# Eight heads to a value product, a 96-column shift product, and a new order of the work, in a four-layer cross-attention kernel

## The reference, cut to what matters

```python
x = _L0_xattn_ref(ctx, x, ...)        # causal attention 0, cross 1, relu feed-forward
x = _L1_xattn_ref(x, ctx, ...)        # causal attention 2, cross 3, experts
x = _L2_xattn_ref(x, ctx, mask, ...)  # masked attention 4, cross 5, relu feed-forward
x = _L3_xattn_ref(x, ctx, ...)        # cross attention 6
# one attention:
scores = jnp.einsum('bhqd,bhkd->bhqk', q, k) / np.sqrt(HEAD_DIM).astype(np.float32)
if mask is not None:
    scores = jnp.where(mask == 0, NEG, scores)
attn = jax.nn.softmax(scores, axis=-1)
out = jnp.einsum('bhqk,bhkd->bhqd', attn, v)
```

## Time and profile before

| | us |
|---|---|
| median of 3 runs | 3417.2 (3404.26 to 3429.27) |
| profiled execution | 3387.68 |
| its span, first to last instruction | 3385.9 |
| PE busy in the span | 3120.8 |
| DVE busy | 1568.8 |
| ACT busy | 1541.6 |
| POOL busy | 872.8 |
| mean granted clock | 0.951 |

### The profile page before, as it was taken

One profiled execution on the slowest core, in us unless ns is written; L12 is line 12 of the kernel. 1 busy time (PEld: TensorE's weight loads), 2 busy tenths in 40 slices (PEclk: granted clock), 3 DMA queues, 4 the chain that ended last, 5 costly groups with the idle time before them and its releaser, 6 DMA issues. The chain is left out here.

```text
span 3385.9 us, 61962 instructions
## 1 busy us (share of the span) xinstructions
PE 3120.8 (92%) x24016; PEld 2469.1 (73%) x24016; DVE 1568.8 (46%) x4051; ACT 1541.6 (46%) x3403; POOL 872.8 (26%) x991
## 2 busy tenths in 40 slices
PE   6899998999999999975999999789999999999996
PEld 5777776777877777764888888657676776777774
DVE  4544556645566555443100010275555555655542
ACT  3555455555556554442222222245555554555542
POOL 2112214222224222322000000332243433343332
PEclk8999999999999999995999999899999999999996
DMA  9725436455454453742766655553354565453321
GB/s 159 104 40 66 56 49 105 67 71 67 64 74 80 70 67 59 168 77 105 231 220 211 204 198 195 103 82 48 54 76 59 64 77 69 63 80 59 52 54 28
DMA packets 394608, 319.35 MB, mean 94 GB/s; under 512 B 151711, under 2 KB 378271, under 8 KB 394303
## 3 DMA queue, kind: packets, MB, share of 16 engines
q1 hardware_dynamic: 371062, 276.77, 46.7%
q0 software_dynamic: 8272, 23.73, 2.6%
q10 hardware_dynamic: 14981, 14.89, 1.4%
HBM read 134.33 MB, written 37.22 MB: 51 GB/s over the span
## 5 line engine op out<-in xcount | busy, mean ns | idle before, releaser
L1067 DVE TENSOR_REDUCE a_maxima<-a_bank 128x2 f32<-128x512 f32 (+3 forms) x576 | 342.4, 646 | 159.6 <-PE a_bank L690 158.9
L918 ACT ACTIVATE a_prob<-a_bank 128x512 f32<-128x512 f32 (+1 forms) x640 | 335.6, 603 | 157.9 <-PE a_bank L710 154.5
L954 ACT ACTIVATE b_group_hidden<-b_bank,b_b 128x256 f32<-128x256 f32 x312 | 131.0, 471 | 421.7 <-PE b_bank L776 421.7
L918 ACT ACTIVATE c_prob<-c_bank 128x512 f32<-128x512 f32 (+1 forms) x512 | 264.6, 599 | 112.6 <-PE c_bank L710 112.1
L1067 DVE TENSOR_REDUCE c_maxima<-c_bank 128x2 f32<-128x512 f32 (+1 forms) x448 | 260.4, 636 | 112.0 <-PE c_bank L690 110.8
L821 PE MATMUL a_bank<-a_causal_b,keep_identb 128*128 128x256 bf16 (+1 forms) x768 | 251.4, 327 | 46.2 <-DMA a_qs<-a_shift 19.1
L776 PE MATMUL b_bank<-b_group_xt,b_w 128*128 128x256 f32 x1248 | 284.3, 381 | 0.8 <-DVE b_group_xt L1108 0.8
L760 PE MATMUL b_bank<-b_w,b_group_hidden 128*128 128x256 f32 x1248 | 275.8, 379 | 0.9 <-ACT b_group_hidden L954 0.9
L760 PEld LDWEIGHTS b_bank<-b_w,b_group_hidden 128*128 128x128 f32 x1248 | 237.0, 190 | 33.5 <-ACT b_group_hidden L954 1.3
L776 PEld LDWEIGHTS b_bank<-b_group_xt,b_w 128*128 128x128 f32 x1248 | 235.6, 191 | 32.0 <-DVE b_group_xt L1108 1.2
L1113 DVE TENSOR_TENSOR b_group_y<-b_bank,b_b 128x512 f32<-128x512 f32 x39 | 27.0, 691 | 364.7 <-PE b_bank L760 364.7
(11 more groups left out here) (237 smaller groups left out, 6692.4 us busy)
## 6 DMA issues: line engine op xcount, KB each, us to landing
b_w<-in_L_xattn_e_w SPq DMA_DIRECT2D x78, 1024.0 KB, 7.2
a_qs<-a_parts_q SPq DMA_DIRECT2D x384, 128.0 KB, 4.9
c_qs<-c_parts_q SPq DMA_DIRECT2D x288, 128.0 KB, 6.9
a_ks<-a_parts_k SPq DMA_DIRECT2D x192, 128.0 KB, 6.0
c_ks<-c_parts_k SPq DMA_DIRECT2D x96, 128.0 KB, 5.9
b_group_x<-sorted_in SPq DMA_DIRECT2D x39, 256.0 KB, 6.6
sorted_out<-b_group_y ACTq DMA_DIRECT2D x39, 256.0 KB, 5.1
sorted_in<-a_zeros SPq DMA_DIRECT2D x8, 1024.0 KB, 9.7
```

The source lines that it names most:

```text
L918: act.activation(prob[0:rows, first:first + cols], bank[0:rows, 0, 0:cols], ACT.Exp, scale=SCALE).then_inc(k.own(s), 1)
L954: ins = act.activation(hidden[:, f, :], bank[:, 0, j * S:(j + 1) * S], ACT.Gelu, bias=b1[:, f:f + 1])
L1067: v.tensor_reduce(maxima[:, q:q + qn, h:h + n].rearrange("p q h -> p h q"), bank[:, 0, 0:cols].rearrange("p (j q n) -> p j q n", j=n, q=qn ...
```

## The change

Five edits. The first two touch what TensorE executes, the others only the lists.

1. "pv" takes eight heads: one step in place of two, which comes after the exps of both groups, holds two `prob` tiles and fills its bank alone. The matmuls are the same.
2. "turn_shift" gives TensorE 96 columns in place of 48: its own query tile's parts and the next one's. For the second tile the neighbour is a zeroed block that `least` gets (six memsets on DVE, three in each phase). Rows 48 to 95 of the result are not read.
3. `Plan.run` adds 0.1 us to the start of a TensorE step when the step before it was a value product and this one is not, or the other way round.
4. The offset in the urgency is now looked up by stage, and by stage and attention (or norm); norms, maxima and the mask's "cut" are new stages.
5. `AHEAD` has new numbers (38 entries, of which one line is shown).

```diff
@@ Plan.run
-            urgency = {k: way / per_sequence - self.steps[k].b + (ahead or {}).get(self.steps[k].kind, 0.0)
+            urgency = {k: way / per_sequence - self.steps[k].b + (ahead(self.steps[k]) if ahead else 0.0)
                        for k, way in urgency.items()}
...
             (start, _, _), k = best
+            columns = self.steps[k].kind == "pv"
+            if self.steps[k].engine == "tensor" and columns != in_columns:
+                in_columns, start = columns, max(start, free_at["tensor"] + 0.1)
@@ attend_steps
-        plan.step("tensor", "pv", b, at, g, us=0.6 if at in CAUSAL else 0.7 if at in SELF else 0.27,
-                  after=[("exp", b, at, (g, len(units) - 1)), ("value", b, at)], behind=[("pv", b, at, g - 1)] if g else [],
-                  takes=["bank", "raw"] if g % 2 == 0 else [], gives=["prob"] + (["values"] if g == H // 4 - 1 else []),
-                  bank=pv, prob=prob, values=values, raw=raw)
...
+            plan.step("tensor", "pv", b, at, i, us=1.13 if at in CAUSAL else 1.35 if at in SELF else 0.5,
+                      after=[("exp", b, at, (g - 1, len(units) - 1)), ("exp", b, at, (g, len(units) - 1)), ("value", b, at)], behind=[("pv", b, at, i - 1)] if i else [],
+                      takes=["bank", "raw"], gives=["prob0", "prob1"] + (["values"] if g == H // 4 - 1 else []),
+                      bank=pv, prob0=probs[0], prob1=probs[1], values=values, raw=raw)
@@ AHEAD
-         "c": {"enters": 1.9, "projs": 0.2, "shifts": 0.7, "scores": 1.1, "pvs": -0.1, "ends": 0.1, "ffs": -0.7, "gains": -4.3}}
+         "c": {"shifts": 0.8, "ends": 0.1, ("ends", 4): -0.3, "enters": 2.2, "ffs": -0.7, ("ffs", 6): 0.5,
...
@@ tensor_program, turn_shift
-                ins = pe.matmul(bank[0:NPART * H, 0, q * P:(q + 1) * P], least["parts"][:, q, :, :].rearrange("p s h -> p (s h)"),
-                                k.identb, start=True, stop=True)
+                ins = pe.matmul(bank[0:2 * NPART * H, 0, q * P:(q + 1) * P],
+                                least["parts"][:, q:q + 2, :, :].rearrange("p q s h -> p (q s h)"), k.identb, start=True, stop=True)
@@ lane_pools
-    k.tiles["least"] = [{"parts": c.sb(f"least{i}_parts", [P, QT, NPART, H], BF16), "rest": c.sb(f"least{i}_rest", [P, QT, H])}
+    k.tiles["least"] = [{"parts": c.sb(f"least{i}_parts", [P, QT + 1, NPART, H], BF16), "rest": c.sb(f"least{i}_rest", [P, QT, H])}
...
+    for least in k.tiles["least"]:
+        c.fill(least["parts"][:, QT, :, :], 0.0)
```

More of the change, by code:

```diff
@@ L422, in start_steps @@
     plan.step("vector", "fold", -1, "a", us=0.4, after=[("load", -1, "a", "rows")])
[L426 to L429, removed]
+STAGES = {"enters": ("enter", "ctx_load"), "norms": ("stats", "moments", "eps", "rstd", "apply"), "turns": ("turn", "turned"),
+          "projs": ("proj", "high", "rest", "middle", "low", "copy"), "values": ("value_proj", "value"), "maxima": ("qm", "max"),
+          "shifts": ("shift_high", "shift_rest", "shift_middle", "shift_low", "turn_shift", "turned_shift", "shift_in"),
+          "scores": ("km", "exp", "cut"), "pvs": ("pv",), "ends": ("raw", "turn_raw", "recip", "weigh", "turn_normed", "heads"),
@@ L430 @@
           "outs": ("out", "add"), "ffs": ("ff", "relu"), "gains": ("bias", "gain", "shift")}
-AHEAD = {"a": {"enters": -2.0, "turns": -0.6, "projs": 0.8, "values": -0.4, "scores": 0.1, "pvs": -0.5, "ends": 0.3, "outs": -0.9,
-               "ffs": 3.1},
-         "c": {"enters": 1.9, "projs": 0.2, "shifts": 0.7, "scores": 1.1, "pvs": -0.1, "ends": 0.1, "ffs": -0.7, "gains": -4.3}}
+STAGE_OF = {kind: stage for stage, kinds in STAGES.items() for kind in kinds}
+NORM_OF = {"l0_1": 0, "l0_2": 1, "l0_3": "l0_ff", "l1_0": 2, "l1_1": 3, "l1_3": 4, "l2_1": 5, "l2_2": "l2_ff", "l2_3": 6}
@@ L436, in ahead_of @@
 def ahead_of(phase):
-    return {kind: by for stage, by in AHEAD[phase].items() for kind in STAGES[stage]}
+    by = AHEAD[phase]
+    return lambda s: (by.get(STAGE_OF.get(s.kind), 0.0) + by.get((STAGE_OF.get(s.kind), NORM_OF.get(s.at, s.at)), 0.0))
 def weights_in(plan, at):
@@ L714, in tensor_program @@
         elif s.kind == "pv":
[L715 removed]
+            values, groups = tile(s, "values").rearrange("p t h c -> p t (h c)"), (2 * s.part, 2 * s.part + 1)
             until.wait_ge(*done("fill", -1, phase))
             until.wait_ge(*done("value", b, at))
[L718 to L727 removed]
+            until.wait_ge(*max(done("exp", b, at, (g, len(key_units(at, g)) - 1)) for g in groups))
+            until.wait_ge(*freed(s, "bank"))
+            last = len(key_tiles(at)) - 1
+            for base, g in zip((0, S), groups):
+                prob = tile(s, "prob0" if base == 0 else "prob1")
+                for kt, kn in enumerate(key_tiles(at)):
+                    for j in range(4):
+                        first, q0 = prob_columns(at, j, kt)
+                        ins = pe.matmul(bank[32 * j:32 * j + 32, 0, base + q0:base + S],
+                                        values[0:kn, kt, (4 * g + j) * (HD + 1):(4 * g + j) * (HD + 1) + 32],
+                                        prob[0:kn, first:first + S - q0], start=(kt == 0), stop=(kt == last),
+                                        tile_position=(0, 32 * j))
             ins.then_inc(k.own(s), 1)
@@ L926, in scalar_program @@
         elif s.kind == "raw":
[L927 removed]
+            until.wait_ge(*done("pv", b, at, s.part))
             until.wait_ge(*freed(s, "raw"))
@@ L1072, in vector_program @@
             until.wait_ge(*freed(s, "least"))
-            v.tensor_scalar(least["parts"][:, :, 0, :], tile(s, "maxima"), -1.0, None, ALU.mult).then_inc(k.own(s), 1)
+            v.tensor_scalar(least["parts"][:, 0:QT, 0, :], tile(s, "maxima"), -1.0, None, ALU.mult).then_inc(k.own(s), 1)
         elif s.kind == "shift_rest":
@@ L1076, in vector_program @@
             until.wait_ge(*done("shift_high", b, at))
-            v.scalar_tensor_tensor(least["rest"], tile(s, "maxima"), -1.0, least["parts"][:, :, 0, :],
+            v.scalar_tensor_tensor(least["rest"], tile(s, "maxima"), -1.0, least["parts"][:, 0:QT, 0, :],
                                    ALU.mult, ALU.subtract).then_inc(k.own(s), 1)
@@ L1081, in vector_program @@
             until.wait_ge(*done("shift_rest", b, at))
-            v.tensor_copy(least["parts"][:, :, 1, :], least["rest"]).then_inc(k.own(s), 1)
+            v.tensor_copy(least["parts"][:, 0:QT, 1, :], least["rest"]).then_inc(k.own(s), 1)
         elif s.kind == "shift_low":
```

29 lines of the change are left out of this document (12 added, 17 removed).

## The result

The changed kernel takes 3308.5 us (median of 4 runs, 3307.31 to 3322.73), the kernel before took 3411.1 beside it: ratio 0.970, 95% interval 0.965 to 0.975. The direction was right, the size wrong.

A forecast was written before the change was run, and what follows sets the result against it. TensorE's own list was taken to bound the kernel (PE busy 3120.8 of 3385.9 us). Visits -46, 96 columns +3, attention 5 -10, attention 4 +3 sum to -50: 3417.2 - 50 = 3367 us, range 3325 to 3405.

The forecast's parts named there:

- Edits 4 and 5, a new order.: TensorE's list: attention 5's earlier shift DMA in phase c -10 us, attention 4's "out" to next turn +3, phase a nothing.
- Phase a: nothing, bounds -15 and +15: New order in phase a: PE work between producer and user shorter in some places, longer in others; nothing, bounds ±15 us.
- Edits 1 and 3, fewer visits: TensorE: 165 fewer changes from full width to narrow products, 44 fewer inner changes, 98 fewer slow first rounds: -46 us.
- Edit 2's price: turn_shift at 96 columns: taken as full width, with longer weight loads partly hidden; +3 us, bounds nothing and 6.
- Exps to pv: Last score to the pair's pv: exps end 2.2 us later, PE has 3.4 and 2.5 us other work; no wait.
- Attention 4's out to the next turn: Phase c: PE's other work falls from 7.7 to 3.9 us against a 3.65 us chain; +3 us, bounds 0 and 10.
- The waits go too: Rival: attention 5's waits go altogether and phase c's 22 us of clock loss too; -86 us, 3331, chance 0.18.
- The gain turns into waiting: Rival: half of the 46 us is lost to DMA and DVE waits, order gives nothing; -20 us, 3397, chance 0.18.
- The pairs come late: Rival: pv needs eight heads' exps, PE stops there if ACT falls behind; 0.4 us each, +90, 3457, chance 0.07.
- 96 columns are not full width: Rival: turn_shifts keep their visits, only the value products' 98 go; -33 us, 3384, chance 0.05.
- three signs of being wrong: turn_shift still shows 0.09 both sides; PE waits for prob at L738 over some 10 us; PE idle grows over 20.

The follow-up runs named there:

- e5: The changed kernel with the old urgency offsets, edits 1, 2 and 3 kept: ratio 0.9899 to the kernel before.
- e10: Edits 1, 2 and 3 with the new urgency offsets in phase c alone, the old ones in phase a: ratio 0.9763 to the kernel before.
- e11: Edits 1, 2 and 3 with the new urgency offsets in phase a alone, the old ones in phase c: ratio 0.9828 to the kernel before.
- e2: The kernel before with edit 2 alone (turn_shift 96 columns wide), all lists as before: ratio 0.9934 to the kernel before.
- e3: The kernel before with edit 1 alone (value products of eight heads as one step), old offsets, no charge, 48 columns: ratio 0.9972.
- e8: The kernel before with the shift's DMA of phase c issued by ScalarE right behind its copy, TensorE's list the same: ratio 0.9913.
- e12: The changed kernel with the planner's charge for a change of tiling at 0.2 us in place of 0.1: ratio 0.9975 to the kernel before.
- e6: The changed kernel with turn_shift 48 columns wide again, its five lists untouched: ratio 0.9731 to the kernel before.
- e1: The kernel before, unchanged, profiled a second time beside timed runs: ratio 0.9997, profiled execution 3404.7 us.
- e7: The changed kernel without the planner's 0.1 us charge at changes (edit 3 out): ratio 0.9948 to the kernel before.
- e17: The changed kernel with the planner multiplying DMA landing times by 1.33 in place of 1.35: ratio 0.9931 to the kernel before.
- e15: The changed kernel with the shift's DMA issued by ScalarE in both phases: ratio 0.9559 to the kernel before.

## Why the prediction was wrong in size

**The step that failed is "Edits 4 and 5, a new order."** It was entered at -10 and +3 in phase c and nothing in phase a, with bounds of 15 there. The new offsets measured 67 us, good to 18, with edits 1 to 3 in place (e5 to the changed kernel): 46 in phase c, 24 in phase a (e10, e11). Its method was to go through places where PE waits and compare the work between producer and user. That found a right place, and what it said there came out well: the DMA ahead of the small copies, 0.8 us after the turn for my 1.1, and attention 5's waits 6 us shorter for my 10. All waits for c_shift, which I put at 15 to 25 us, are 29.8, though. And it leaves out three things.

- *The other waits.* I priced the new order against the waits of the kernel before, one place at a time. Edits 1 to 3 with the old offsets have a list of their own (e5), and PE idles for 282 us in it. From there to the changed kernel the profiles have 35 us less idling, 6 less cost of the clock and 6 less net; 28 of the 35 lie in phase c. The three waits that fell most there, e5 first, with the same steps at other lines:

```profile
PE c_bank L714 <- DMA c_qs<-c_shift: 37.4, 12, 6.5
PE c_bank L663 <- DVE c_tok L1055: 12.8, 8, 2.6
PE c_bank L702 <- DVE c_least_parts L1092: 9.7, 7, 2.9
```

```profile
PE c_bank L722 <- DMA c_qs<-c_shift: 29.8, 13, 7.2
PE c_bank L671 <- DVE c_tok L1063: 7.4, 3, 3.9
PE c_bank L710 <- DVE c_least_parts L1100: 2.6, 3, 1.4
```

- *The clock.* I had put its loss in c at 22 us and left it to a rival. The cost fell from 119 to 90 over the program, but e5 has 96: most of this fall is there without the new offsets, and by which edit it came is open (e2 has 124, e3 114). In c eight of before's ten waits at attention 5 stood beside a stretch at the lower level. In the changed kernel two of ten do; the 1.81 us wait of the timeline above has 1.00 behind it, the longest two 0.77 and 0.73:

```profile
2743.00:2750.00 7.00, 6.48 (x44) 5.22 (x46) 2.39 (x4) 4.46 (x10) 0.00 (x0) 1.00 0.21 11
2811.20:2818.50 7.30, 6.68 (x34) 5.61 (x36) 0.92 (x2) 4.69 (x10) 0.00 (x0) 0.77 0.19 10
...
2538.70:2545.00 6.30, 6.00 (x34) 4.92 (x36) 1.53 (x3) 4.75 (x10) 2.30 (x2) 0.73 0.83 58
```

  e8 shows that shorter waits at attention 5 pay by themselves: with PE's list untouched, waits 10 us shorter in sum took phase c from 1230.5 to 1209.4 us.
- *The spread of lists.* "Phase a: nothing, bounds -15 and +15" had no row behind it. Lists that do the same matmuls with the same visits lie 2.7% apart (changed and e12). 253 us of idling and 119 of clock were there to be won or lost, and that was the bound I should have kept for a step that replaces every list.

**"Edits 1 and 3, fewer visits": right.** -46 forecast; net fell by 42 to 45 (40 to 43 compared alike), e2 gave 17 to 20 for its 19, e6 18 for 22, e3 17 to 20 for 25. In e5, without the new offsets, 34 us of it reached the time.

**"Edit 2's price": right in size, below what can be told.** A 96-column load takes 124 ns where the 48-column one took 102:

```profile
L710 PEld LDWEIGHTS c_bank<-keep_identb,c_least_parts 128*96 128x96 bf16 x96 | 10.2, 124 | 8.9 <-DVE c_least_parts L1100 6.4 <-issue 0.6
```

At 22 ns more in 224 loads it would be 5 us if none were hidden. The 40 ns more that the prediction estimated by the Trainium skill ("TensorE: Matmul & The Clock Gate", "LDWEIGHTS (loading the stationary operand)") do not show.

**"Exps to pv": right. "Attention 4's out to the next turn": not borne out.** PE waits for prob at L738 for 6.4 us in all. The turns of phase c wait 7.4 us for c_tok (above), for 11.1 before and 9.1 in e1, where I had added 3:

```profile
PE a_bank L738 <- ACT a_prob L932: 4.2, 4, 2.1
...
PE c_bank L738 <- ACT c_prob L932: 2.2, 4, 0.7
```

**The rivals.** "The waits go too" named the clock and came nearest, but the waits did not go: 17.6 of 23.7 us are left, and eight of the ten have no slow stretch behind them. Its 22 us of clock in phase c were too many (the cost there fell from 46 to 31 us, or from e1's 40) and it had none in phase a (70, in e1 78, to 56). "The gain turns into waiting" names something that happens: e3, e7, e12 and e17 gave back some 7 to 25 us, two fifths to three quarters of what net had won. But fewer visits do not do it by themselves: e5, with the old offsets, gave back only some 5 us of 39, and e2 nothing. It depends on the list that comes out. "The pairs come late" and "96 columns are not full width" are refuted. None of the three signs of being wrong that I had named appeared: all three watch for a loss, none for a gain that is larger.

**What stays open.** Which of the 38 new numbers make the gain, and which places of phase a hold its 24 us, since its sequences overlap without a steady pattern (its last 90 us are one: the clock cost 20 us there before, 21 in e5 and 9 in the changed kernel); and why the shift's DMA takes 6 to 10 us from issue to scores beside other copies when it took 2.7 to 4.5 us at the end of phase c. That it is the large copies just ahead was argued from the lists, not tried alone.

## What to carry to other kernels

- Where a planner orders the work, price the edit to the work (here -40 to -45 us, good to a few us) apart from the new list. For the list keep bounds as wide as the engine's idle time and its loss at the lower clock allow, unless neighbouring lists have been timed; disturb a planner number that stands for nothing in both kernels before crediting or blaming a rule.
- A wait on the engine that sets the time costs its length and, in many cases here, a slow stretch beside it. Shortening a recurring wait can pay even where it does not go; and the first thing to look at is which queue issues the DMA and behind what (here 1.4 points from another issuing engine).

## What the runs showed of the hardware

- In phase c of the changed kernel attention 5's waits of 1.20 to 2.05 us left the granted clock at 1.00, and those of 2.13 and 2.34 us had the lower level behind them. It is not the wait's length alone: waits of 1.66 and 1.67 us in the kernel before and of 1.76 us in e8 had the lower level beside them, and waits of 2.89 us before, 1.87 us in e8 and 2.34 us in e15 had not. In e7 eight waits of 2.7 to 5.9 us stood beside 6.8 us of it each.
- A change between full width and 32-column tiles costs TensorE some 0.09 us each way plus a slow step behind the earlier trace rows; counted over whole kernels (165 visits, 40 to 45 us) it holds. The 48-column product was a change too (0.22 us), the 96-column one is not (0.15 us, and the step ahead at its plain length).
- The same 24 KB DMA took 2.8 us from issue to its user at the end of the changed kernel, with the DMA engines nearly idle (share 0.01 from 3270 to 3280 us), 8.2 us in the timeline above (share 1.01 from 2725 to 2745 us), and 10.3 us in e7. Issued from ScalarE's queue instead of SyncE's in phase a, its waits fell from 45.4 to 18.0 us, though ScalarE has 1541.9 us of work itself.
